# Two neighbouring steps' low parts made in one GpSimd subtraction of 1024 columns, in every second pair of steps, in a fused attention and feed-forward kernel

## What is computed

```python
x = x + _layernorm(_L0_attn_ref(_layernorm(x), Wq, bq, Wk, bk, Wv, bv, Wo, bo, gamma, beta))
x = x + _layernorm(_L0_ffn_ref(_layernorm(x), w_gate, w_up, w_down))

# _L0_attn_ref: 16 heads of 64
q = jnp.einsum('bsd,dhk->bshk', x, Wq) + bq      # k and v likewise
scores = jnp.einsum('bqhk,bshk->bhqs', q, k) * scale
attn = jax.nn.softmax(scores, axis=-1)
ctx = jnp.einsum('bhqs,bshk->bqhk', attn, v)
y = x + jnp.einsum('bqhk,hkd->bqd', ctx, Wo) + bo
return (y - mu) * jax.lax.rsqrt(var + EPS) * gamma + beta

# _L0_ffn_ref: silu(x Wg) * (x Wu), then Wd, weights are integers / 127
```

## Time and profile before

| | before |
|---|---|
| median of three runs | 2808.67 us |
| the profiled execution's own time | 2810.7 us |
| its span in the profile | 2808.9 us |
| TensorE clock granted, mean | 0.989 |
| TensorE busy with matmuls | 96% of the span |
| ScalarE, VectorE, GpSimd busy | 87%, 83%, 81% |
| the 32 heads' steps | from about 90 to 2437 us |

### The profile page before, as it was taken

One profiled execution on the slowest core, in us unless ns is written; L12 is line 12 of the kernel. 1 busy time (PEld: TensorE's weight loads), 2 busy tenths in 40 slices (PEclk: granted clock), 3 DMA queues, 4 the chain that ended last, 5 costly groups with the idle time before them and its releaser, 6 DMA issues. The chain is left out here.

```text
span 2808.9 us, 83179 instructions
## 1 busy us (share of the span) xinstructions
PE 2698.2 (96%) x34176; PEld 1727.5 (61%) x34176; DVE 2341.5 (83%) x4203; ACT 2447.0 (87%) x4760; POOL 2274.6 (81%) x1919
## 2 busy tenths in 40 slices
PE   5899999999999999899999999999999999989997
PEld 2466666666666666556666666666666666656764
DVE  4688888999998998768888889999999998678785
ACT  3799999999999999889999999999999999846553
POOL 3799999999989999789999899999999999613232
PEclk8999999999999999999999999999999999999998
DMA  3322123212211111122221222221111122321210
GB/s 101 75 56 53 40 52 75 45 41 41 41 36 39 36 40 40 39 81 58 54 46 44 53 53 41 41 42 41 41 40 40 37 42 70 99 76 46 91 53 23
DMA packets 207100, 144.89 MB, mean 52 GB/s; under 512 B 157824, under 2 KB 181632, under 8 KB 206720
## 3 DMA queue, kind: packets, MB, share of 16 engines
q1 hardware_dynamic: 206720, 139.58, 20.6%
HBM read 51.20 MB, written 37.88 MB: 32 GB/s over the span
## 5 line engine op out<-in xcount | busy, mean ns | idle before, releaser
L536 POOL TENSOR_TENSOR p_l<-p_f,p_h 128x512 f16<-128x512 f32 x1536 | 1946.2, 1295 | 92.9 <-ACT p_h L610 90.2
L663 DVE TENSOR_REDUCE mx<-ps_aux 128x1 f32<-128x512 f32 x2048 | 1349.5, 681 | 303.9 <-PE ps_aux L834 295.8
L609 ACT ACTIVATE p_f<-ps_score 128x512 f32<-128x512 f32 x2048 | 1271.7, 622 | 18.1 <-PE ps_score L863 17.9
L610 ACT ACTIVATE p_h<-ps_score 128x512 f16<-128x512 f32 x2048 | 1280.9, 627 | 0.0
L888 PEld LDWEIGHTS ps_ctx<-v_hi_one_lo,p_h 128*128 128x128 f16 x16384 | 891.4, 97 | 245.3 <-POOL p_l L536 1.2
L888 PE MATMUL ps_ctx<-v_hi_one_lo,p_h 128*128 128x65 f16 (+1 forms) x16384 | 920.8, 193 | 1.5 <-POOL p_l L536 0.9
L888 PE MATMUL ps_ctx<-v_hi_one_lo,p_l 128*128 128x65 f16 x8192 | 791.2, 192 | 0.0
L862 PE MATMUL ps_score<-q_hilo,k_hihi 128*128 128x512 f16 x2048 | 778.2, 380 | 7.4 <-ACT v_new L568 5.4
L863 PE MATMUL ps_score<-q_hi_max,k_lo_one 65*128 65x512 f16 x2048 | 780.1, 381 | 0.0
L834 PE MATMUL ps_aux<-k_hihi,q_hilo 128*128 128x512 f16 x2048 | 620.5, 382 | 21.7 <-DVE mx L663 13.7
L681 DVE TENSOR_TENSOR p_l<-p_f,p_h 128x512 f16<-128x512 f32 x512 | 536.3, 1048 | 22.6 <-ACT p_h L610 22.6
(11 more groups left out here) (174 smaller groups left out, 2163.4 us busy)
## 6 DMA issues: line engine op xcount, KB each, us to landing
v_heads<-v_new SPq DMA_DIRECT2D x64, 258.0 KB, 2.0
v_hi_one_lo<-v_heads SPq DMA_DIRECT2D x32, 516.0 KB, 6.0
heads<-ctx_n SPq DMA_DIRECT2D x128, 128.0 KB, 2.0
x_all<-heads SPq DMA_DIRECT2D x8, 2048.0 KB, 8.7
k_hihi<-hi_st SPq DMA_DIRECT2D x62, 256.0 KB, 4.4
q_hi_max<-hi_st SPq DMA_DIRECT2D x32, 256.0 KB, 3.6
k_lo_one<-lo_st SPq DMA_DIRECT2D x32, 256.0 KB, 4.3
q_hilo<-hi_st SPq DMA_DIRECT2D x31, 256.0 KB, 3.2
```

The source lines that it names most:

```text
L536: nc.gpsimd.tensor_tensor(p_l[:, r], p_f[:, r], p_h[:, r], ALU.subtract).then_inc(lo_pool, 1)
L609: nc.scalar.activation(p_f[:, r], ps_score[:, bank], ACT.Exp, scale=exp_scale)
L610: nc.scalar.activation(p_h[:, r], ps_score[:, bank], ACT.Exp, scale=exp_scale).then_inc(exp_done, 1)
L663: nc.vector.reduce_max(mx[:, blk % 2, tt, ch:ch + 1], ps_aux[:, n % SIDE], AX_X).then_inc(max_read, 1)
```

## The change

GpSimd's rule for the four steps of a quad is a table, `LOW_WIDTH`. For t % 4 == 0 it subtracts one slot, as before. For t % 4 == 1 nothing, as before (VectorE's step). For t % 4 == 2 it now does nothing. For t % 4 == 3 it waits for the exponentials of step t, subtracts the two slots of steps t - 1 and t in one instruction of 1024 columns, and adds 2 to lo_pool. TensorE's waits keep their counts, and VectorE's part is the same.

```diff
+LOW_WIDTH = (1, 0, 0, 2)
...
             def head(g, u, maxima, items):
                 for t in range(STEPS):
-                    if not lo_on_dve(t):
-                        r = t % PROBS
+                    wide = LOW_WIDTH[t % 4]
+                    if wide:
+                        slots = slice(t % PROBS + 1 - wide, t % PROBS + 1)
                         pool.wait_ge(exp_done, g * STEPS + t + 1 + RING)
-                        nc.gpsimd.tensor_tensor(p_l[:, r], p_f[:, r], p_h[:, r], ALU.subtract).then_inc(lo_pool, 1)
+                        nc.gpsimd.tensor_tensor(p_l[:, slots], p_f[:, slots], p_h[:, slots], ALU.subtract).then_inc(lo_pool, wide)
```

## The result

The changed kernel took 2997.14 us, the median of four runs (2995.05 to 3001.78), against 2808.79 us: a ratio of 1.0671, with a 95% interval from 1.0654 to 1.0688. It is 188 us slower, where 32 us were forecast; the time lies outside the range given, beyond the rival in which the even quads are caught too (2970 us). The profiled execution took 2995.05 us, of which 2993.3 is span.

The account below looks back on a forecast made before the run. The prediction took TensorE's matmuls to pace the kernel. Its terms, 21 + 5 + 1 + 4 + 1 = 32 us on the profiled 2810.7 us, gave 2843 us, or 2841 us against the median; range 2811 to 2880 us.

Parts of the forecast that it names:

- even quads are caught too: Rival: in even quads VectorE also comes second, 0.8 us lost every second quad; 2970 us, a third 2895; chance 0.17.
- What bounds the kernel: The 32 heads are paced by TensorE's matmuls; GpSimd's saving of 95 us is worth nothing.
- The wide instruction's length: GpSimd's merged subtraction of 1024 columns takes 2.13 us, where one of 512 takes 1.16.
- The exclusion lasts for the whole instruction: VectorE and GpSimd subtractions exclude each other; whoever comes second waits until the other's whole instruction is over.
- `weigh` isn't late: Low parts of steps 4q+2 and 4q+3, ready 2.2 us after the exponential, make `weigh` wait nowhere inside heads.
- In an even stretch it doesn't occur ... Cost nothing: In even quads VectorE subtracts before the wide instruction starts, so the added wait is absent and costs nothing.
- the regular place: Quad 7, after the weight split of step 24, is where VectorE regularly arrives after the wide instruction has begun.
- The chain of quads 7 to 9: VectorE's subtractions at steps 29, 33 and 37 wait for wide ones: 1.4 us in each of 15 heads, 21 us.
- heads 1 to 4 and 17 to 20: Heads with values, where a value lies between and gives VectorE time: 0.16 us each, 1 us in all.
- the margin of 0.14 us: In even quads the wide instruction would start 0.14 us after VectorE's subtraction, too late to be first.
- Head 15: ScalarE's value waits for GpSimd's low part behind the wide subtraction at five places: 4 us, bounds 0 and 5.
- The end of head 31: After the last exponential, `weigh` of step 63 starts later behind the wide subtraction: 1.2 us, with nothing beside it.

Follow-up runs that it names:

- experiment 3: The changed kernel, with VectorE reducing p_f to one column in place of its subtraction (low parts of steps 4q+1 left out): 2823.44 us, 1.0052.
- experiments 13: The changed kernel with wide subtractions only in quads 1 to 6, 10, 13 and 14 of each head, single ones elsewhere: 2840.33 us, 1.0113.
- experiment 14: The changed kernel with single subtractions in quads 0, 11 and 15 of each head, wide ones in the other 13: 2869.27 us, 1.0217.
- experiment 4: The changed kernel with two single subtractions in quads 11 and 15 of each head, wide ones in the other 14: 2925.74 us, 1.0416.

## Why the forecast was wrong, point by point

- **What bounds the kernel**: right. TensorE paced it, and GpSimd's saving was worth nothing.
- **The wide instruction's length**, 2.13 us: right. In experiment 3, where little excludes it, its mean is 2133 ns.
- **The exclusion lasts for the whole instruction**: right. VectorE's longest subtraction is 2620 ns, and the reduction with one SBUF input never waits.
- **`weigh` isn't late**: right inside the heads. The wait went through the maxima.
- **"In an even stretch it doesn't occur ... Cost nothing", and quad 7 as "the regular place"**: this is the step that failed. It is true of an even stretch: quads 1 to 6 cost nothing in experiments 13 and 14. But the heads don't begin even. The prediction lists the subtraction and the weight split's w_h as VectorE's instructions that exclude GpSimd. It names neither the cast of a projection between two heads nor the negation at the head's start; in head 25 of the kernel before they had taken 0.78 and 0.21 us. With a wide instruction before them they take 1.76 and 1.18 us, VectorE enters each head late, and its subtractions of quads 1 to 6 are late in place of those of quads 7 to 9.
- **The chain of quads 7 to 9**, 1.4 us a head: right as a mechanism, a little small. With even heads before it (experiment 14) it gives 1.7. VectorE ended its three subtractions 2.83, 2.82 and 2.82 us after the exponentials there, where I had 2.76. One step in it was wrong without effect: I let VectorE come 0.2 us earlier at quad 7 and left out w_l, which takes 1.26 us there (0.43 before); VectorE came 1.10 us after the exponential and not 0.37, but the wide one's end decides. But only 15 heads were counted: heads 1 to 4 and 17 to 20, which I had at 0.16 us, lost 0.9 each, and heads 7 to 9 up to 8. So it is 60 us in experiment 14, head 15 included, in place of 32.
- **The rival "even quads are caught too"** was the case, by another door. I had it enter by the margin of 0.14 us being lost; the margin held, and the casts and the negation broke it. Its chance of 0.17 was too low for a process that, once started, keeps itself going until something gives VectorE time. Its price was good: 0.8 us in every second quad forecast, 0.9 in every two measured. But its sum was added up in two ways: 2970 us for all quads leaves out the forecast's own 32 us, and 2895 for a third of them has them in. With them, all quads would give 3001 us.
- **Head 15**, 4 us with a bound of 5: mis-sized, 6.1 measured. The copy is 1.04 us later at such a place and not 0.75; it showed nothing to spare there.
- **The end of head 31**, 1.2 us: right by the trace, not tried by itself. From the end of the last exponential to the start of `weigh` of step 63 it is 2.70 us, and was 1.42.

Three kernels that differ by a step each divide the 188 us. The weight split's chain, head 15, heads 7 to 9 and the small places, with the ordinary heads begun even, make 60 us (experiment 14). Quad 0's wide one, through the negation behind it, adds 56 (experiment 4 less 14). The wide ones of quads 11 and 15, behind which casts stand, add 71 (the changed kernel less experiment 4). How the last part divides among the casts of a head wasn't tried; in the traces 44 of the 71 us are lost in quads 13 and 14, behind the wide one of quad 11. No kernel here that computes all low parts beat the kernel before.

## What to carry to other kernels

Where two engines exclude each other for whole instructions, the length of one engine's instruction is the other's longest wait, so merging instructions on an engine that has time to spare can cost the one that hasn't. To size it, list every instruction of the other engine that takes part in the exclusion, the small ones too, and ask of each what the longer wait does to the next turn; one late arrival can be handed on from turn to turn. A stretch that is even in the trace is no safe price for a loop with such a feedback: ask what puts it out of step and what puts it back, and how often.

## What the runs showed of the hardware that I had not expected

- A negation of four columns (128x4, 0.16 us by itself) and a cast of 512 columns (0.41 us) on VectorE wait for GpSimd's subtraction just as the two-input subtraction does: 2.11 and 1.86 us at the most in the changed kernel. Both had waited before the change too, up to 1.09 and 0.78 us.
- A reduction of p_f, one SBUF input to one column, took 668 to 689 ns beside GpSimd instructions of up to 2149 ns, 512 times without a wait.
